# A gating loop on one core: next batch turned back first, then this batch's gate products with feature blocks as weights

## What is computed

```python
def attention_end(z):              # over all of z: batch norm, then a gate
    zn = (z - mean(z, (0, 2))) * rsqrt(var(z, (0, 2)) + EPS) * gamma + beta
    return sigmoid(relu(zn))
# second block
out = crucial_features * A_S1 + subcrucial_features * A_S2
x = x + out
# third block
h = layernorm(x)
gate_logits = einsum('bsh,he->bse', h, gate_w)      # 8 experts
top_vals, top_idx = top_k(gate_logits, 2)
w_e = softmax(top_vals) scattered to the experts
x = x + einsum('bseo,bse->bso', einsum('bsh,eho->bseo', h, expert_w), w_e)
```

## Time and profile before

| | us |
|---|---|
| median of 3 runs | 1209.61 (1209.42 to 1210.43) |
| the profiled execution | 1210.52 |
| its span | 1208.5 |
| PE busy in it | 1041.2 (86%) |
| VectorE busy | 577.8 (48%) |
| ScalarE busy | 393.7 (33%) |
| GpSimd busy | 486.3 (40%) |
| mean granted TensorE clock | 0.913 of 2.4 GHz |

### The profile page before, as it was taken

How to read it: one execution, slowest core, us unless ns; L and a number is a source line. 1 busy time by engine, 2 the same in 40 slices (tenths; PEclk the granted TensorE clock), 3 DMA queues, 4 the chain that set the end, 5 groups by cost and what they waited for, 6 DMA issues and landing times. The chain is left out here.

```text
span 1208.5 us, 13393 instructions
## 1 busy us (share of the span) xinstructions
PE 1041.2 (86%) x3476; PEld 547.7 (45%) x3482; DVE 577.8 (48%) x1645; ACT 393.7 (33%) x1124; POOL 486.3 (40%) x661
## 2 busy tenths in 40 slices
PE   6786888888888779798764699999999999999995
PEld 6784444554544435423324344444444444444442
DVE  5636588888787868978766212111121111111110
ACT  2435768676666217757630000000000000000000
POOL 3825576646565100006510534443334343334431
PEclk9877899888888889998885699999999999999998
DMA  8310120100000132002567236455544647363432
GB/s 305 115 53 0 46 79 1 53 36 1 1 1 1 71 139 71 1 1 87 209 269 288 69 70 208 79 139 164 158 120 107 180 90 213 69 208 73 90 77 39
DMA packets 38461, 120.25 MB, mean 100 GB/s; under 512 B 6219, under 2 KB 9350, under 8 KB 38406
## 3 DMA queue, kind: packets, MB, share of 16 engines
q1 hardware_dynamic: 25590, 79.77, 17.9%
q0 software_dynamic: 12816, 39.86, 15.1%
HBM read 82.91 MB, written 36.70 MB: 99 GB/s over the span
## 5 line engine op out<-in xcount | busy, mean ns | idle before, releaser
L1969 PE MATMUL bank<-T,X 128*128 x1184 | 511.4, 594 | 14.0 <-DVE X L2007 10.8
L1969 PEld LDWEIGHTS bank<-T,X 128*128 128x128 f32 x1184 | 225.4, 191 | 299.2 <-issue 299.2
L2021 DVE TENSOR_SCALAR X<-bank,col_p 128x512 f32<-128x512 f32 x37 | 27.8, 751 | 409.6 <-PE bank L1969 409.6
L1987 ACT ACTIVATE X<-bank,col_p 128x512 f32<-128x512 f32 x37 | 25.4, 687 | 524.0 <-PE bank L1969 524.0
L1922 POOL DMA_INDIRECT X<-x_nrm,col_s x156 | 149.5, 958 | 92.6 <-issue 47.2
L1931 POOL DMA_INDIRECT out_dram<-X,col_d x37 | 60.0, 1622 | 269.4 <-DVE X L2021 255.1
L450 POOL TENSOR_TENSOR T<-T 128x8 f32<-128x8 f32 x216 | 94.4, 437 | 16.3
L634 PE MATMUL bank<-nat,T 128*128 128x512 f32 x128 | 88.1, 841 | 12.1 <-ACT X L787 5.4
L799 ACT ACTIVATE M<-X,T 128x256 bf16<-128x256 f32 x200 | 98.4, 495 | 0.0
L459 POOL TENSOR_TENSOR rs<-ve,neg_half 128x4 f32<-128x4 f32 x36 | 38.5, 1069 | 105.3 <-DVE ve L942 105.1
L217 POOL TENSOR_TENSOR late<-late,neg_half 128x1 f32<-128x1 f32 x32 | 17.5, 549 | 130.2 <-DVE late L213 130.2
(11 more groups left out here) (320 smaller groups left out, 1434.0 us busy)
## 6 DMA issues: line engine op xcount, KB each, us to landing
T<-in_L_ffn_expert_w_dram SPq DMA_DIRECT2D x8, 4096.0 KB, 17.6
out_dram<-X SPq DMA_DIRECT2D x17, 512.0 KB, 3.8
M<-in_x_dram SPq DMA_DIRECT2D x16, 512.0 KB, 7.2
X<-in_x_dram SPq DMA_DIRECT2D x16, 512.0 KB, 5.0
x_nrm<-H SPq DMA_DIRECT2D x16, 512.0 KB, 3.3
T<-in_ctx_dram SPq DMA_DIRECT2D x9, 512.0 KB, 3.8
X<-x_nrm,col_s POOLq DMA_INDIRECT x156, 3.6
X<-in_ctx_dram SPq DMA_DIRECT2D x4, 512.0 KB, 7.0
```

The source lines that it names most:

```text
L1969: mm = nc.tensor.matmul(bank[2 * u + n][:, :], xgt[u][:, k, :], Tf[:, ds(odd * (KD * D) + (k * D + n * BANK), BANK)], start=(k == 0), stop ...
```

## The change

Of the first parts, the second half of chunk 2 moves from in front of the pooled products to behind the batch norm, and the second half of chunk 3 moves behind back(0). In the loop PE does back(b+1) ahead of second_part(b). second_part takes blocks of T (128 features x 128 tokens) as weights and gate_w (8 columns) as what is moved, 16 products a batch in place of 8, and leaves the sums with tokens on the lanes. So second_turned, gathered, band's use for it and the semaphores l_cp and l_tp go. VectorE gates batch 0 ahead of the first two copies of first sums, and copies sums 2 and 3 behind residual(0). The five operations on known move from b = 1 to b = 2.

```diff
--- before.py
+++ after.py
@@ -1343,11 +1343,9 @@
         w_in_sem = [sem(f"w_in{w}") for w in range(2)]
         nrm_st = [sem(f"nrm_st{u}") for u in range(2)]
         gmul, gm_first, gm_done, back_mm, x2_done = (sem(n) for n in ("gmul", "gm_first", "gm_done", "back_mm", "x2_done"))
-        l_mm, l_cp, l_tp, l_set, ln_nb, p1_cp, p1_tp, gs_mm = (sem(n) for n in ("l_mm", "l_cp", "l_tp", "l_set", "ln_nb", "p1_cp", "p1_tp", "gs_mm"))
-        BACK, P1_BANK, P2_SUMS, P2_BANK = (0, 1, 6, 7), 2, (3, 4), 5
-        band_rows = band[:, :, :].rearrange("p c n -> p (c n)")
+        l_mm, l_set, ln_nb, p1_cp, p1_tp, gs_mm = (sem(n) for n in ("l_mm", "l_set", "ln_nb", "p1_cp", "p1_tp", "gs_mm"))
+        BACK, P1_BANK, P2_BANK = (0, 1, 6, 7), 2, 3
         by_expert = [fin[0:E, u, :] for u in range(2)]
-        by_expert2 = [band_rows[0:E, u * S:(u + 1) * S] for u in range(2)]
 
         def expert_src(e):
             return expert_w[e, :, :].rearrange("(k p) n -> p k n", p=P)
@@ -1422,7 +1420,7 @@
                         products(pe, t + LAG)
                     if t != 1 and t < NT:
                         turned(t)
-                    if NT - LAG <= t < NT + LAG:
+                    if NT - LAG <= t < NT + LAG - 1:
                         c, part = divmod(t - (NT - LAG), 2)
                         first_part(pe, c, part * KU, (part + 1) * KU)
 
@@ -1443,7 +1441,8 @@
                 nc.tensor.matmul(bank[1][:, 0:2], ones[:, :], gsum[:, :], start=True, stop=True).then_inc(g_pe, 1)
                 pe.wait_ge(g_dve, 6)
                 nc.tensor.matmul(bank[6][:, 0:2], ones[:, :], gsum[:, :], start=True, stop=True).then_inc(g_pe, 1)
-                first_part(pe, 3, 0, KD)
+                first_part(pe, 2, KU, KD)
+                first_part(pe, 3, 0, KU)
 
                 def back(b):
                     for n in range(2):
@@ -1463,35 +1462,26 @@
                     mm.then_inc(p1_tp, 1)
 
                 def second_part(b):
-                    if b >= 2:
-                        pe.wait_ge(l_cp, b - 1)
-                    else:
-                        pe.wait_ge(p1_cp, b + 2)
-                    for k in range(KD):
-                        mm = nc.tensor.matmul(bank[P2_SUMS[b % 2]][0:E, 0:S], gate[:, k, :], T[:, k, b * S:(b + 1) * S], start=(k == 0), stop=(k == KD - 1))
-                    mm.then_inc(l_mm, 1)
-
-                def second_turned(b):
                     if b == 0:
-                        pe.wait_ge(p1_cp, 4)
-                    pe.wait_ge(l_cp, b + 1)
+                        pe.wait_ge(p1_cp, 2)
                     for h in range(CT):
                         t = CT * b + h
-                        mm = nc.tensor.transpose(bank[P2_BANK][:, t * E:(t + 1) * E], by_expert2[b % 2][:, h * P:(h + 1) * P], ident[0:E, 0:E])
-                    mm.then_inc(l_tp, 1)
-
+                        for k in range(KD):
+                            mm = nc.tensor.matmul(bank[P2_BANK][:, t * E:(t + 1) * E], T[:, k, t * P:(t + 1) * P], gate[:, k, :], start=(k == 0), stop=(k == KD - 1))
+                    mm.then_inc(l_mm, 1)
+
+                back(0)
+                first_part(pe, 3, KU, KD)
                 first_turned(0)
                 first_turned(1)
                 nc.tensor.matmul(bank[P1_BANK][:, NT * E:NT * E + E], ones[:, :], g_part, start=True, stop=True).then_inc(gs_mm, 1)
                 for b in range(B):
-                    back(b)
+                    if b + 1 < B:
+                        back(b + 1)
                     if b == 0:
                         first_turned(2)
                         first_turned(3)
-                    else:
-                        second_turned(b - 1)
                     second_part(b)
-                second_turned(B - 1)
 
             @block.scalar
             def _(act):
@@ -1666,37 +1656,30 @@
                     hold(dve, ln_rstd, NT + t + 1)
                     v.scalar_tensor_tensor(back_of(1, t), mean_of(1, t), -1.0, rstd_of(1, t), ALU.mult, ALU.mult).then_inc(ln_nb, 1)
 
-                def gathered(b):
-
-                    hold(dve, l_mm, b + 1)
-                    if b >= 2:
-                        hold(dve, l_tp, b - 1)
-                    v.tensor_copy(by_expert2[b % 2], bank[P2_SUMS[b % 2]][0:E, 0:S]).then_inc(l_cp, 1)
-
                 def first_sums(c):
                     if c >= 2:
                         hold(dve, p1_tp, c - 1)
                     hold(dve, p1_mm, c + 1)
                     v.tensor_copy(by_expert[c % 2], bank[P1_SUMS[c]][0:E, :]).then_inc(p1_cp, 1)
 
+                for n in range(2):
+                    gated_half(v, 0, n, lambda s_, c_: hold(dve, s_, c_)).then_inc(gm_first, 1)
                 first_sums(0)
                 first_sums(1)
-                for n in range(2):
-                    gated_half(v, 0, n, lambda s_, c_: hold(dve, s_, c_)).then_inc(gm_first, 1)
+
                 def behind(b):
                     for h in range(CT):
                         back_shift(CT * b + h)
-                    gathered(b)
 
                 for b in range(B):
+                    residual(b)
                     if b == 0:
                         first_sums(2)
                         first_sums(3)
-                    residual(b)
-                    if b > 0:
+                    else:
                         behind(b - 1)
                     stats(b)
-                    if b == 1:
+                    if b == 2:
                         dve.wait_ge(gs_mm, 1)
                         then(v.tensor_copy(g_all, bank[P1_BANK][:, NT * E:NT * E + E]))
                         dve.wait_ge(p1_tp, 4)
@@ -1707,7 +1690,7 @@
                 behind(B - 1)
                 then(v.tensor_tensor(shift, over_e(mean_all(1)), over_t(g_all), ALU.mult))
                 then(v.tensor_tensor(known, known, shift, ALU.subtract))
-                dve.wait_ge(l_tp, B)
+                dve.wait_ge(l_mm, B)
                 then(v.tensor_tensor(known, known, bank[P2_BANK][:, 0:NT * E].rearrange("p (t e) -> p t e", e=E), ALU.add))
                 then(v.tensor_tensor(logits[:, :, :], known, over_e(rs_all(1)), ALU.mult))
```

## The result

| | before | changed |
|---|---|---|
| median of 4 runs | 1210.02 (1209.42 to 1211.29) | 1194.86 (1190.67 to 1199.91) |
| the profiled execution | 1210.52 | 1194.41 |
| its span | 1208.5 | 1192.4 |
| the long run of L1306 starts (32 rows before, 24 changed) | 525.26 | 525.42 |
| residual of batch 1 starts | 560.73 | 561.41 |

The ratio is 0.9861, interval 0.9828 to 0.9893: faster by 15.2 us. That is 1.4%, less than 2% but clear of the noise. The forecast was 1203.9 with a range of 1196.5 to 1212.0.

What follows compares the result with a forecast made beforehand. It took the PE-DVE hand-over of each batch as the bound, and PE in the new loop. Start +0.3, loop -7.3 and tail +1.3 made -5.7 us, so 1203.9 us, range 1196.5 to 1212.

Steps and rivals of the forecast that it cites:

- What bounds the stretch: From 525 to 635 us, PE and DVE hand one batch to and fro; a us won there is one overall.
- The batch norm: Ahead of the gating loop: moving eight rows starts the pooled products 2.5 us earlier, at 536.6.
- that is used up: Rows and copies behind the batch norm take back its 2.5 us earlier start; batch 1's residual starts 0.3 later.
- the stated sum: Net change before the loop, at the start of batch 1's residual: +0.3 us.
- The prices of rows: Loop costs per batch: 32 narrow rows 3.7 or 7.0 us by clock, transposes 1.9 or 3.7, DVE some 7.0.
- p: Share of PE's loop work at the low clock, taken as 0.6; PE's batch is 5.6 + 5.1p us.
- the term of -7.3: Gating loop: six periods of 8.7 us, PE the bound, take 52.0 us against 59.2 before.
- my first rival: Gating loop: DVE becomes the bound at a high clock, periods of 7.0 us, 1194.0 us in all; chance 0.15.
- The tail: After the last residual: waiting for the last gate products delays the weight loads, 16.1 us against 14.8, so +1.3.
- slower, by the clock: Gating loop: narrow products and short transposes keep PE at 1.2 GHz, period 10.7 us, 1219.4 us in all; chance 0.12.

Runs made afterwards that it cites:

- the form alone: Kernel before with only the gate products changed to T blocks as weights, no copy or second turn, loop order and first parts as before: 1218.90 us, ratio 1.0047.
- the lighter shifts: Changed kernel with VectorE's back shifts as operations with one SBUF input: 1203.45 us, ratio 0.9926 to the kernel before.

## Why the prediction was right in direction and wrong in bound and size

**What bounds the stretch** held: the hand-over of a batch between PE and VectorE was the cost, and its end moved the whole time one to one (48.7 us from the weights to the expert loop in both).

**The batch norm** held as far as it was forecast: L1432 starts at 536.73 (forecast 536.6), the first statistics at 557.84 (557.4), batch 1 0.5 later (0.3). But "that is used up" compared with the kernel before. Against the new loop without the move it was worth 3.6, of which 1.5 is the start; the stated sum is not touched by that.

**The prices of rows** held: 32 narrow rows 3.7 and 6.8 us (3.7 and 7.0), transposes 1.97 and 3.65 (1.9 and 3.7), VectorE 6.1 and 0 to 0.8 for GpSimd's hold (0 to 2.3, taken as 0.9).

**The step that failed is p**, the share of PE's work at the low clock, and with it the term of -7.3. I took 0.6, "just under the share of narrow work", which makes 8.7 us a batch and PE the bound. The runs show about half of that. PE's batch without a gap is 7.02 (586.43 to 593.45), and 5.6 + 5.1p gives that at p = 0.28; by the rows it is the transposes, 1.9 of 5.6 us of work, that run low, and the narrow rows that run high, the opposite of what I had assumed. The mean clock of 0.73 from 561 to 605 us means low for half of the time, but a share of time is not a share of work: the low half does less of it. At 0.28 PE is level with VectorE, and VectorE became the bound. Six periods were 43.25 against the 52.0 of the forecast: -16.0, not -7.3.

That 43.25 is the 43.3 of my first rival is luck. The rival had six periods of 7.0 and 1.3 for the operations on known, at a clock that stays high. Measured are 10.57 in the period with these operations, 2.3 more than its 8.3, and 32.7 in the five others, 2.3 less than its 35.0.

I took p from the kinds of work as if the clock answered to each row at once. The windows show that it answers later: in the changed kernel it rises when the transposes are nearly over and falls when the products are. That the products enjoy what the transposes before them brought, and the transposes pay for the products, is my reading and not shown, for the same rows in the same order stay at 1.2 GHz altogether with the form alone and with the lighter shifts. Why the clock falls well in one and not in the other stays open, but for the slip told above. With these rows the loop was seen in two states, some 7.0 and 10.14 us a batch, and the 8.7 of an average p is neither.

**The tail** was the other error: +1.3 forecast, nothing measured. The last transposes were over before the last residual began, where I had put 2.0 us of them behind it, and the 64 narrow rows took 10.7 where I had 11.4. They ended 9.8 us behind the start of that residual, not 13, so the old path (a store that must land before nring is free) stayed the later one.

**The rival "slower, by the clock"** was put at 0.12. It was not what this kernel did, but the form alone did it, as far as the clock goes. Its 1219.4 lies near the 1218.9 measured there by luck: that kernel's six periods are 60.8 where the rival had 64.2, the weights are issued 12.9 behind the last residual where it had 16.7, and 5.3 us of the profiled run lie ahead of the stretch. The rule of the Trainium skill that I had beside it (TensorE: Matmul & The Clock Gate, Part 4, the high clock does not engage for transposes) does not hold here: between 563 and 604 us PE ran nothing but transposes and rows of 8 columns, and the granted clock came back to 1.00 six times. Nor does the price in section LDWEIGHTS of that page of the Trainium skill, columns / 1.2 ns or 107 ns for 128 columns, fit at the low clock: 32 rows took 6.83 us, where it would give 3.4.

## What to carry to other kernels

Where two engines hand each batch to and fro, let one start the next batch ahead of finishing this one; that alone gave 10.8 of the 15.5 us of the stretch. When a change swaps wide products for narrow ones, don't average the clock over them: look in the trace which rows run at which clock, and treat the low-clock loop as a state of its own that a small edit elsewhere, even a faster engine, can bring on. Compare by a stretch of the trace when the runs vary more ahead of the change than by it.

## What the hardware showed that I had not expected

- A lighter VectorE made the kernel 8.6 us slower (1203.45 against 1194.87 in median; the stretch grew by 9.1), and 24 more rows a batch on PE cost another nothing (stretch 110.1 against 110.2): both through TensorE's clock.
- With the form alone PE was busy without a gap for 71 us (565 to 636) and stayed at 1.2 GHz, with 16 transposes of 128 columns in every 48 rows.
- An operation of 128x1 with one SBUF input ran in 0.33 for two beside GpSimd's multiplication, where the form with two inputs took 1.02 for two, and 3.07 in one place. The Trainium skill (SBUF — State Buffer, section SBUF: two separate sides) says that an operation of VectorE with two SBUF inputs and a GpSimd operation that reads SBUF exclude each other; for VectorE's side the traces agree.
